# Multi-query loops: products with the values in runs of four chunks, spread of the reciprocals ahead of the rows

## The reference, cut to what matters

```
q = (xn @ Wq).reshape(b, n, H, DH).transpose(0, 2, 1, 3) * scale
k = concatenate([nk, k]); v = concatenate([nv, v])      # one key and value set for all heads
sim = einsum('bhid,bjd->bhij', q, k) + bias             # H = 16, DH = 64, n = 1024
sim = where(causal_mask, neg, sim); sim = where(mask, sim, neg)
attn = softmax(sim, axis=-1)
out = einsum('bhij,bjd->bhid', attn, v)
...
return layernorm(out @ Wo, g_out)
```

## Time and profile before

| | |
|---|---|
| median of 3 runs | 3218.07 us |
| profiled execution, its span | 3218.2 us |
| instructions | 50056 |
| PE busy | 2924.2 us, 91% |
| DVE busy | 1882.8 us, 59% |
| ACT busy | 1578.7 us, 49% |
| POOL busy | 382.5 us, 12% |
| mean granted PE clock | 0.953 |

### The profile page before, as it was taken

The page is one execution under the profiler, slowest core; times in us unless marked ns, Lnnn a source line. Parts: engine busy times, 40 slices in busy tenths (PEclk is TensorE's granted clock), DMA queues, the critical chain, the costliest instruction groups (busy, mean ns, idle before and its releaser), DMA issues. The chain is left out here.

```text
span 3218.2 us, 50056 instructions
## 1 busy us (share of the span) xinstructions
PE 2924.2 (91%) x17179; PEld 2052.1 (64%) x17181; DVE 1882.8 (59%) x4554; ACT 1578.7 (49%) x3849; POOL 382.5 (12%) x729
## 2 busy tenths in 40 slices
PE   7978999899999998758799999998999999959996
PEld 5746666546777777344577777764667777836664
DVE  5456555346777766777577777345667777332223
ACT  4403555426666661644466666233566666213331
POOL 4560000001111100000000000000111111012222
PEclk8998999999999999879899999998999999979998
DMA  4452221245444321005432321006544443341112
GB/s 123 121 171 64 44 55 28 76 158 162 124 146 145 121 88 39 1 20 160 130 86 68 86 68 35 20 10 195 171 138 126 150 125 104 118 159 34 34 35 92
DMA packets 242482, 308.23 MB, mean 96 GB/s; under 512 B 27261, under 2 KB 185085, under 8 KB 242096
## 3 DMA queue, kind: packets, MB, share of 16 engines
q1 hardware_dynamic: 235082, 285.50, 29.1%
q0 software_dynamic: 7152, 19.54, 2.1%
HBM read 231.31 MB, written 73.21 MB: 95 GB/s over the span
## 5 line engine op out<-in xcount | busy, mean ns | idle before, releaser
L2407 ACT ACTIVATE cond_p<-cond_p,cond_negm 128x128 f32<-128x128 f32 (+7 forms) x768 | 593.2, 775 | 408.4 <-DVE cond_negm L2438 407.5
L2388 PE MATMUL ps_o<-cond_pt,cond_v 128*64 128x256 f32 (+1 forms) x3840 | 478.2, 370 | 5.1 <-DVE attn_out L2474 0.5
L2368 PE MATMUL ps_s<-cond_k_high,cond_q_high 128*128 128x512 f32 (+5 forms) x1152 | 439.4, 387 | 16.8 <-DVE cond_negm L2438 8.3
L2438 DVE CUSTOM_DVE_ANT_0 cond_p<-ps_s,cond_side,cond_null_scores 128x128 f32<-128x128 f32 (+7 forms) x512 | 403.7, 811 | 28.1 <-PE ps_s L2369 22.6
L2369 PE MATMUL ps_s<-cond_k_both,cond_q_both 128*128 128x512 f32 (+5 forms) x1152 | 394.1, 344 | 0.0
L2378 PE MATMUL ps_t<-ident,cond_p 128*128 128x128 f32 x2304 | 348.8, 281 | 6.8 <-ACT cond_pt L2412 4.8
L2388 PEld LDWEIGHTS ps_o<-cond_pt,cond_v 128*64 128x64 f32 x3840 | 237.4, 136 | 180.4 <-issue 89.8
L2378 PEld LDWEIGHTS ps_t<-ident,cond_p 128*128 128x128 f32 x2304 | 250.0, 140 | 106.0 <-issue 77.1
L1507 ACT ACTIVATE attn_pt<-ps_t 128x512 f32<-128x512 f32 (+3 forms) x384 | 173.0, 490 | 237.9 <-PE ps_t L1468 174.6
L2368 PEld LDWEIGHTS ps_s<-cond_k_high,cond_q_high 128*128 128x128 f32 x1152 | 219.9, 191 | 40.1 <-DVE cond_negm L2438 22.3
L2446 DVE COPY cond_pt<-ps_t 128x512 f32<-128x512 f32 (+1 forms) x240 | 140.4, 585 | 166.3 <-PE ps_t L2378 164.6
(11 more groups left out here) (503 smaller groups left out, 4682.1 us busy)
## 6 DMA issues: line engine op xcount, KB each, us to landing
mqa_q_halves<-cond_q_cut SPq DMA_DIRECT2D x96, 512.0 KB, 4.7
cond_q_both<-mqa_q_halves SPq DMA_DIRECT2D x384, 128.0 KB, 3.2
cond_q_high<-mqa_q_halves SPq DMA_DIRECT2D x192, 128.0 KB, 3.0
cond_side<-in_fside_16xSxS SPq DMA_DIRECT2D x32, 512.0 KB, 7.2
moe_experts<-in_L_ffn_W SPq DMA_DIRECT2D x16, 1024.0 KB, 12.2
cond_side<-in_fside_16xSxS SPq DMA_DIRECT2D x32, 448.0 KB, 5.6
cond_side<-in_fside_16xSxS SPq DMA_DIRECT2D x32, 384.0 KB, 5.0
cond_side<-in_fside_16xSxS SPq DMA_DIRECT2D x32, 320.0 KB, 4.6
```

The lines of the kernel that those rows point to most:

```text
L2368: nc.tensor.matmul(out, c32(a.Q1[i][:, h, s * P:(s + 1) * P]), c32(a.K1[:, keys]), start=True, stop=False)
L2388: last = nc.tensor.matmul(sums[u % ON][h * HD:(h + 1) * HD, s0 * P:2 * P], a.V[:, b * QB + kb, :], PT[c % PT_SLOTS][:, (2 * h + s0) * P:(h ...
L2407: nc.scalar.activation(p, p, ACT.Exp, bias=negm[u % SMALL][:, r:r + 1], scale=-1.0, accum_out=rsum[u % SMALL][:, r:r + 1]).then_inc(exped, 1)
L2438: nc.vector.tensor_tensor_reduce(out=probs(u, r, 0, q + 1), in0=m.S[k % 2][:, row_offset(L):row_offset(L) + L], in1=toep_back(u, h, L) if ...
```

## The change

Only `mqa_order` changes, in two ways. A new list `ripe` holds chunks whose attends are due. Chunks are collected in `waiting` until there are four of them or the unit ends, then they become ripe, and all ripe chunks are attended in the next group, behind its first rows. So attends come in runs of four or two chunks of one unit; before they came two by two. The spread is put directly behind the turns of the group and ahead of its rows, when its den is two groups old or when the ripe chunks hold the last one of its unit. The other steps keep their order. At the end of the list the chunks left are the ripe ones.

```
--- before.py
+++ after.py
@@ -1625,7 +1625,7 @@
 
     places, need = mqa_ring()
     rows = [(u, r) for u in range(len(MQA_UNITS)) for r in range(4)]
-    steps, spreads, waiting = [], [], []
+    steps, spreads, waiting, ripe = [], [], [], []
     ahead, finished, chunk, n_groups = 0, -1, 0, 0
 
     def place(limit, most):
@@ -1662,14 +1662,18 @@
                 spreads.append((n_groups, u))
             if g == q0:
                 finished = u
+            closing = [c[0] for c in ripe if c[1] == MQA_UNITS[c[0]][2] + 1]
+            while spreads and (n_groups - spreads[0][0] >= 2 or spreads[0][1] in closing):
+                steps.append(("spread", spreads.pop(0)[1]))
             place(ROWS_AHEAD, 2)
-            if spreads and n_groups - spreads[0][0] >= 2:
-                steps.append(("spread", spreads.pop(0)[1]))
-            while len(waiting) > 4:
-                attend(waiting.pop(0))
+            for c in ripe:
+                attend(c)
+            ripe = []
+            if len(waiting) == 4 or g == q0:
+                ripe, waiting = waiting, []
             place(ROWS_AHEAD, len(rows))
             n_groups += 1
-    for c in waiting:
+    for c in ripe:
         attend(c)
     return steps
```

## The result

The changed kernel takes 3232.11 us (median of 9 runs, 3226.82 to 3236.91), the kernel before 3219.67 us in the same comparison. The ratio is 1.0033 with a 95% interval of 1.0022 to 1.0045: 7 to 14 us slower. The forecast was 3246 us, slower by 28 us. The direction was right, the size was more than twice too large.

The account below looks back on a forecast made before the run. PE was taken to bound the loops. Per period 28.39 - 1.0 - 0.15 + 0.75 + 0.85 + 0.1 = 28.94 us; over 16 periods and 3 loops +26 us, plus 2 for the side matrix: 3246 us, range 3190 to 3270.

Parts of the forecast that it names:

- (a): Third chunk's turn behind a run: PE arrives early and waits for ScalarE's copy behind an exponential; 0.75 us per period.
- The saved visits: PE's visits to the 64-column value products fall from 10 to 6 per period, saving 1.0 us per period.
- The early spread: Spread copied before the exponentials, so VectorE's stop before the output product goes; saves PE 0.15 us per period.
- (b): Short rows of the next q0 = 0 unit: third and fourth wait for VectorE's work; 0.85 us per period.
- (c): Last turns of unit 23: PE, a visit earlier, waits for ScalarE's copy; 0.1 us per period.
- (d): First and third loops: PE waits longer before the spread, as POOL waits for the side matrix; +2 us in all.
- The rival built on it: Spread ahead of rows waits for the late side matrix, rows queued behind; 24 us on top, 3270 us; chance 0.20.

Follow-up runs that it names:

- e5: The changed kernel with each group's exponentials moved behind the next group's two turns and the short rows split over two groups; 3190.3 us, ratio 0.9901.
- e8: The kernel before, visits of two chunks, with only the exponentials moved behind the next group's two turns; 3195.4 us, ratio 0.9912.
- e2: The kernel before with only the spread moved ahead of the rows, products still in visits of two chunks; 3221.2 us, ratio 0.9995.
- e1: The changed kernel with its runs, but the spread back behind the first rows of its group; 3327.8 us, ratio 1.0327.
- e4: The changed kernel with the exponentials of a group's rows moved behind the next group's two turns; 3194.6 us, ratio 0.9912.
- e6: The changed kernel with exponentials behind the next group's two turns and the spread back behind its group's rows; 3182.4 us, ratio 0.9873.
- e7: The changed kernel with exponentials behind the next turns, spread back behind the rows and short rows split over two groups; 3166.2 us, ratio 0.9831.
- e9: The kernel before with exponentials behind the next group's turns and value products 128 columns wide, outputs not the reference's; 3422.4 us, one run.

## Why the prediction was partly wrong

The mechanism was right: visits are saved, three waits appear, and they outweigh the saving. The step that failed is (a): the chain of DVE and ACT was taken to run "without a gap for anything on PE", at 9.60 us, and the wait behind it was put at 0.75 us per period. The chain held two waits for PE's own turns, shrank to 9.36 us, and the wait cost 0.54.

**The saved visits, right.** 1.0 us per period was forecast; e5 against e8, neither with the three waits, gives 1.04. That is 0.26 a visit. The forecast had 0.29 for three and 0.1 for the fourth; that the fourth is the cheap one was not measured.

**The early spread, right for visits of two and missed for runs.** 0.15 was forecast, e2 gives 0.19 and e8, which takes the same stop away by ScalarE's order, 0.18. But "DVE is not the bound" was said of the old order. In runs, VectorE's stop sits in the chain that PE waits for, and the part is worth 2.0 us per period, some 96 us in all (e1; its smaller side waits are in this figure). It did not spoil the forecast, since I read the chains with the early spread in place, but the text gave the wrong account of what that part is for.

**(b), right.** 0.85 forecast; 0.71 + 0.13 = 0.84 by the timeline, 0.79 by taking it away (e5 against e4). **(c)**, 0.1 forecast, 0.12 measured.

**(a), the term that failed.** 0.75 forecast; measured 0.48 up to the start of the turn, 0.54 with the slower step behind it. PE's side of it was right: 8.94 us dense between row 22.3 and turn 22.1, and 1720.39 - 1710.98 less the wait of 0.48 gives 8.93. The chain on the other side took 9.36 us in the changed kernel instead of 9.60, and from the copy's end to the turn 0.05 passed instead of the 0.1 that I had from a wait for POOL. The VectorE timeline of the kernel before shows what I passed over:

```profile
904.91 0.69 DVE L2446 COPY cond_pt<-ps_t 128x512 f32<-128x512 f32 x1 [0.78 <-PE ps_t L2378]
905.52 0.15 DVE L2460 TENSOR_TENSOR cond_dn<-cond_rsum,cond_nulle 128x4 f32<-128x4 f32 x1
905.84 1.28 DVE L2438 CUSTOM_DVE_ANT_0 cond_p<-ps_s,cond_side,cond_null_scores 128x1024 f32<-128x1024 f32 x1
```

The reciprocals and the next row stood behind a copy that had waited 0.78 us for PE's turn. The same place after the change (second loop; there the copy had waited 0.80 before it):

```profile
1716.12 0.69 DVE L2450 COPY cond_pt<-ps_t 128x512 f32<-128x512 f32 x1
1717.04 0.16 DVE L2464 TENSOR_TENSOR cond_dn<-cond_rsum,cond_nulle 128x4 f32<-128x4 f32 x1 [0.23 <-ACT cond_nulle L2420]
1717.33 1.25 DVE L2442 CUSTOM_DVE_ANT_0 cond_p<-ps_s,cond_toep,cond_null_scores 128x1024 f32<-128x1024 f32 x1
```

PE, being early, had the turn ready, the copy waits for nothing, and VectorE now waits for ScalarE's null term instead, 0.23. That link of the chain was PE itself, and it moved with PE. From the VectorE operation of row 23.0 to that of row 23.1 it is 2.79 us instead of 2.97 (2.96 in the second loop). The link before it, from row 22.3 to row 23.0, held a like wait of 0.7 us and went from 2.62 to 2.57.

**The sum.** The runs give each term by taking it away: 28.39 - 0.18 (the stop, e8) - 1.04 (the visits, e5 against e8) + 0.79 ((b), e4 against e5) + 0.66 ((a) and (c), the changed kernel against e4) = 28.62. The period was forecast to grow by 0.55 and grew by 0.23. Of the 0.32 between them, (a) is 0.21; the visits and the stop saved 0.04 and 0.03 more, (b) cost 0.06 less and (c) 0.02 more than forecast.

Over 48 periods 0.32 is 15 us. The other differences nearly cancel, which is luck: the side waits grew by 4 us more than forecast, and against that the first and last periods of the loops, costed like the others, came out some 2.5 us shorter and the rest of the kernel 4 us shorter. That leaves 10.8 us between the two profiled executions and 12.4 between the medians, where 28 was forecast.

**(d), the side matrix, too small.** +2 us forecast, 6.3 us in the traces (18.6 to 24.9). The place was right. The rival built on it put 24 us on top, and 4 came. But what it says happens, PE asking for the widened reciprocals with rows queued behind, is real: moving only the spread in front of the rows raises the side waits from 18.6 to 24.4 (before, e2), from 4.0 to 19.7 (e6, e4) and from 12.9 to 45.1 (e7, e5). With the short rows split it decides: e7 is 24 us faster than e5. How much of the changed kernel's 24.9 comes from the spread's place stays open, since its partner e1 (3.1) has periods 2 us longer. These waits differ much between periods of one execution, so single traces give their size only roughly. Why late exponentials shrink them without runs (e8, 18.6 to 7.2) was not tested and stays open.

## What to carry to other kernels

Work saved on the bounding engine shortens the loop only where every wait behind it has slack for the time by which that engine now comes earlier. Walk the new order once, releaser by releaser, and in the chain of the other engines look at each idle time: one that was ended by the engine that you make earlier will shrink with it, only one between the others is rigid. When two parts of a change meet in the strict order of a third engine, cost them together (here -0.19 alone and -2.0 behind the other); and often the cure is to move that engine's own late work (the exponentials) rather than the bounding engine's.

## What the runs showed of the hardware that was not expected

The two matmul records of one product with 64 columns of weights start 7 ns apart, and the next product 0.21 us later; a visit of two chunks, eight records, takes 1.01 us. With 128 columns (e9) the records start 0.22 us apart, and the eight take 1.73 us. So the narrow products pay 0.26 us for each visit and are still much cheaper in this kernel; a period is 28.21 us with them (e8) and 32.92 us without (e9).

In the loops a PE instruction that waited for VectorE's work on a row or for ScalarE's copy of a turn starts 0.055 us behind the end of that work, one that waited for POOL's copy 0.145 us. Behind the waits (a) and (c) four transposes took 0.06 us longer than the 0.44 of four that had not waited.
